# Groups of 8 samples by 64 d in the order of the gather, for a recommendation tower on one core

## The reference

```python
def _cin(x, weights, biases):
    B, F, D = x.shape
    hidden = x
    finals = []
    for i, (w, b) in enumerate(zip(weights, biases)):
        size = w.shape[0]
        z = jnp.einsum('bhd,bfd->bhfd', hidden, x).reshape(B, hidden.shape[1] * F, D)
        y = jnp.einsum('bcd,oc->bod', z, w) + b[None, :, None]
        y = jax.nn.relu(y)
        if i != n_layers - 1:
            hidden, direct = (y[:, :size // 2, :], y[:, size // 2:, :])
        else:
            direct = y
        finals.append(direct)
    return jnp.concatenate(finals, axis=1).sum(-1)
...
h = jnp.concatenate([z, dense_ctx], axis=1)
h = jnp.maximum(h @ W_top1 + b_top1, 0.0)
h = jnp.maximum(h @ W_top2 + b_top2, 0.0)
y = h @ W_top3
```

## Time and profile before

| | |
|---|---|
| three runs | 1093.88, 1093.7, 1091.5 us (median 1093.7) |
| profiled execution, whole | 1092.62 us |
| its span, first to last instruction | 1090.8 us |
| mean granted clock of PE | 0.978 |
| busy: PE / DVE / POOL / ACT | 1025.0 / 944.4 / 915.5 / 734.9 us |
| DMA queue of SP, share of the 16 engines | 70.3%, 192 MB |

### The profile page before, as it was taken

One profiled execution on the slowest core, in us unless ns is written; L12 is line 12 of the kernel. 1 busy time (PEld: TensorE's weight loads), 2 busy tenths in 40 slices (PEclk: granted clock), 3 DMA queues, 4 the chain that ended last, 5 costly groups with the idle time before them and its releaser, 6 DMA issues.

```text
span 1090.8 us, 10701 instructions
## 1 busy us (share of the span) xinstructions
PE 1025.0 (94%) x3493; PEld 651.4 (60%) x3493; DVE 944.4 (87%) x623; ACT 734.9 (67%) x907; POOL 915.5 (84%) x300
## 2 busy tenths in 40 slices
PE   2059999999999999999999999999999999999999
PEld 1025556656666666666666666666666666666664
DVE  4059999999999999999999999999998989888982
ACT  1036666767777677777777777777777777777761
POOL 7526878779999999999999899997989888988890
PEclk9569999999999999999999999999999999999999
DMA  4278777687878787778877878787777877786730
GB/s 137 55 188 200 194 186 184 180 198 190 210 178 205 183 213 187 192 191 199 207 185 192 201 181 208 182 206 194 194 184 194 204 183 187 191 208 184 183 84 1
DMA packets 142074, 196.89 MB, mean 180 GB/s; under 512 B 15858, under 2 KB 57458, under 8 KB 141891
## 3 DMA queue, kind: packets, MB, share of 16 engines
q1 hardware_dynamic: 137922, 192.01, 70.3%
q0 software_dynamic: 4096, 4.20, 1.8%
HBM read 175.18 MB, written 20.97 MB: 180 GB/s over the span
## 4 chain that ended last, share of the span: by engine, by line
PE 86%; DVE 4%; issue 4%; DMA 3%; ACT 2%; SPq 1%; DVEq 0%; ACTq 0%
PE py L610 40%; PE py L626 15%; PE py L616 14%; PE py L617 14%; DVE zf L498 2%; ACT zh L362 2%; PE py L631 1%; DMA xs<-x_dram 1%; DMA x_dram<-xf 1%; DMA xs<-in_L_rec_w 1%; PE pt L592 1%; DVE zl L515 1%; PE py L675 0%; PE pzS L675 0%; DVE zf L459 0%
## 5 line engine op out<-in xcount | busy, mean ns | idle before, releaser
L303 POOL TENSOR_TENSOR zl<-zf,zh 128x2048 fp32r<-128x2048 f32 x168 | 772.3, 4610 | 116.2 <-ACT zh L362 114.2
L498 DVE TENSOR_TENSOR zf<-xs,hid 128x2048 f32<-128x2048 f32 x256 | 583.3, 2283 | 67.1 <-ACT hid L377 51.9
L610 PE MATMUL py<-zf,wf 128*128 128x512 f32 x1072 | 485.2, 596 | 6.5 <-DVE zf L498 6.5
L362 ACT ACTIVATE zh<-zf 128x2048 fp32r<-128x2048 f32 x186 | 354.9, 1908 | 44.5 <-DVE zf L498 41.1
L610 PEld LDWEIGHTS py<-zf,wf 128*128 128x128 f32 x1072 | 203.5, 190 | 214.2 <-issue 194.2
L616 PE MATMUL py<-zh,wh 128*128 128x512 f32 x744 | 293.6, 395 | 8.7 <-ACT zh L362 8.7
L617 PE MATMUL py<-zh,wl 128*128 128x512 f32 x744 | 292.1, 393 | 0.0
L626 PE MATMUL py<-zl,wh 128*128 128x512 f32 x744 | 233.8, 436 | 0.0
L498 DVE TENSOR_TENSOR zf<-xs,px 128x2048 f32<-128x2048 f32 x64 | 146.4, 2288 | 37.8 <-DMA xs<-x_dram 35.9
L626 PEld LDWEIGHTS py<-zl,wh 128*128 128x128 f32 x744 | 135.9, 189 | 59.2 <-issue 29.2
L293 POOL DMA_INDIRECT emb<-in_tbl,idx x128 | 143.1, 1118 | 29.9 <-issue 24.5
(11 more groups left out here) (71 smaller groups left out, 439.8 us busy)
## 6 DMA issues: line engine op xcount, KB each, us to landing
xs<-x_dram SPq DMA_DIRECT2D x640, 256.0 KB
x_dram<-xf SPq DMA_DIRECT2D x64, 320.0 KB
emb<-in_tbl,idx POOLq DMA_INDIRECT x128
xs<-in_L_rec_w SPq DMA_DIRECT2D x2, 512.0 KB
xs<-in_L_rec_w SPq DMA_DIRECT2D x1, 1024.0 KB
wt<-in_W_top SPq DMA_DIRECT2D x1, 512.0 KB
wt1b<-in_W_top SPq DMA_DIRECT2D x1, 256.0 KB
wt1a<-in_W_top SPq DMA_DIRECT2D x1, 128.0 KB
```

The lines of the kernel that those rows point to most:

```text
L303: pool.tensor_tensor(zl[:, q], zf[:, s], zh[:, q].bitcast(F32), ALU.subtract).then_inc(lo["P"], 1)
L362: act.activation(zh[:, q], zf[:, s], ACT.Copy).then_inc(hi, 1)
L498: dve.tensor_tensor(zf[:, slot(u)], left, right, ALU.mult).then_inc(mult, 1)
L610: mm = pe.matmul(y, wf[:, w, h], zf[:, s, h], start=first and h == 0, stop=ends and h == T - 1)
```

## The change

A group is now 8 samples by all 64 d, that is, the layout that a gather leaves. `stage_x`, `turn_x` and `copy_xf` go. Each batch of gathers is stored as it comes (`store_batch`): `x_dram` is now one block per chunk of 128 samples, 160 rows of 32 KB, written in pieces of 256 bytes (one sample's 64 numbers of one field), five copies as before. A group reads from each row its 2 KB, so the rows that it reads lie 32 KB apart. Group 0 of a chunk waits for all stores of the chunk, 17 DMAs for chunk 0 in batches of 12, 12, 6 and 2 fields; later chunks go in batches of three or two fields, one a group. SP's order puts batch g-1's store behind the loads of x0, xt and xd, and it waits there for the batch's gathers. `emb` holds two chunks in place of four.

The sum over d is a reduction of each group's 512 columns to 8 (`sum_1`, `sum_2`), straight from PSUM, in place of adds to accumulators and the later `sum_d`. `py1` has two banks, in place of `pt`.

In group 0, xd is loaded in two halves and product P made in two; PE runs four whole matmuls of weights by weights when px0 is ready and three behind the tail, whose result nobody reads; A of group 0 is whole. SP loads xd of group 1 ahead of x0 of group 1.

The core of the diff, blank lines left out:

```diff
 NC = B // P
-ND = 4
-N = ND * P
-G = NC * D // ND
-GC = D // ND
+NS = 8
+N = NS * D
+G = B // NS
...
 def mode(unit):
     name, g = unit
-    if name in "PD":
+    if name in "PD" or unit == ("A", 0):
...
+FIRST_BATCHES = [(0, 0, 12), (0, 12, 12), (0, 24, 6), (0, 30, 2)]
+PER_PERIOD = [[3] * 10 + [2], [2] * 16, [2] * 16]
+LATER_BATCHES = [(c, sum(PER_PERIOD[c - 1][:i]), n) for c in range(1, NC) for i, n in enumerate(PER_PERIOD[c - 1])]
+BATCHES = FIRST_BATCHES + LATER_BATCHES
+BATCH_SEMS = 4
+STORES = [sum(min(m, REPEATS) for b, _, m in BATCHES if b == c) for c in range(NC)]
+def gathered_count(n):
+    return 16 * sum(BATCHES[i][2] for i in range(n % BATCH_SEMS, n + 1, BATCH_SEMS))
+def batch_of(g):
+    return len(FIRST_BATCHES) + g if g < len(LATER_BATCHES) else None
...
-        emb = sb("emb", [P, F, NC, D])
+        emb = sb("emb", [P, 2, F, D])
...
-            def store_x(k):
-                sp.wait_ge(xf_ready, k + 1)
-                dst = x_dram[k, 0:1, :]
-                sp.dma_start(bass.AP(tensor=dst.tensor, offset=dst.offset, ap=[[N, F], [P, ND], [F * N, REPEATS], [1, P]]),
-                             view(xf, 0, [[0, REPEATS], [1, P]])).then_inc(x_stored, 16)
+            def store_batch(n):
+                c, f, m = BATCHES[n]
+                sp.wait_ge(gathered[n % BATCH_SEMS], gathered_count(n))
+                if m < REPEATS:
+                    for i in range(m):
+                        dst = x_dram[c, f + i:f + i + 1, :]
+                        sp.dma_start(bass.AP(tensor=dst.tensor, offset=dst.offset, ap=[[D, P], [F * P * D, REPEATS], [1, D]]),
+                                     view(emb, (c % 2 * F + f + i) * D, [[0, REPEATS], [1, D]])).then_inc(x_stored[c], 16)
+                else:
+                    for i in range(REPEATS):
+                        dst = x_dram[c, i * F + f:i * F + f + 1, :]
+                        sp.dma_start(bass.AP(tensor=dst.tensor, offset=dst.offset, ap=[[D, P], [P * D, m], [1, D]]),
+                                     emb[:, c % 2, f:f + m, :]).then_inc(x_stored[c], 16)
+            def rows(k, r):
+                return x_dram[k // GC, r:r + 1, N * (k % GC):N * (k % GC) + N]
             def run_of_rows(k, r):
-                src = x_dram[k, r:r + 1, :]
-                return bass.AP(tensor=src.tensor, offset=src.offset, ap=[[N, P], [1, N]])
...
-            def block_rows(k, j, t):
-                src = x_dram[k, 4 * t + j:4 * t + j + 1, :]
-                return bass.AP(tensor=src.tensor, offset=src.offset, ap=[[N, F], [4 * N, T], [1, N]])
+                src = rows(k, r)
+                return bass.AP(tensor=src.tensor, offset=src.offset, ap=[[P * D, P], [1, N]])
+            def block_rows(k, j, t, n=T):
+                src = rows(k, 4 * t + j)
+                return bass.AP(tensor=src.tensor, offset=src.offset, ap=[[P * D, F], [4 * P * D, n], [1, N]])
             def load_x0(k):
-                sp.wait_ge(x_stored, 16 * (k + 1))
+                if k % GC == 0:
+                    sp.wait_ge(x_stored[k // GC], 16 * STORES[k // GC])
...
                     sp.wait_ge(mult, NTH["C", k - 2])
+                if k == 0:
+                    for t in range(0, T, 2):
+                        for j in (0, 2, 1, 3):
+                            sp.dma_start(xd[0][F * j:F * j + F, t:t + 2], block_rows(0, j, t, 2)).then_inc(x_first[t // 2], 16)
+                    return
                 for j in (0, 2, 1, 3):
                     sp.dma_start(xd[k % 2][F * j:F * j + F], block_rows(k, j, 0)).then_inc(xd_in[k % 2], 16)
...
+            for n in range(len(FIRST_BATCHES)):
+                store_batch(n)
             sp.wait_ge(w_turned, 6)
-            store_x(0)
             load_x0(0)
             load_xd(0)
             load_xt(0)
-            store_x(1)
+            load_xd(1)
             load_x0(1)
+            load_xt(1)
             load_xe(0)
-            load_xt(1)
-            load_xd(1)
-            store_x(2)
             for g in range(G):
                 if g + 2 < G:
                     load_x0(g + 2)
                     load_xt(g + 2)
                     load_xd(g + 2)
-                if g + 3 < G:
-                    store_x(g + 3)
+                if g >= 1 and batch_of(g - 1) is not None:
+                    store_batch(batch_of(g - 1))
                 if g + 1 < G:
                     load_xe(g + 1)
...
-            def gather(c, f):
+            def gather(n, i):
+                c, first, m = BATCHES[n]
+                if i >= m:
+                    return
+                f = first + i
+                if i == 0 and c >= 2:
+                    pool.wait_ge(x_stored[c - 2], 16 * STORES[c - 2])
+                if i == 0 and n >= BATCH_SEMS:
+                    pool.wait_ge(gathered[n % BATCH_SEMS], gathered_count(n - BATCH_SEMS))
                 pool.indirect_dma_start(
-                    out=emb[:, f, c, :], out_offset=None, in_=tables[f],
+                    out=emb[:, c % 2, f, :], out_offset=None, in_=tables[f],
                     in_offset=bass.IndirectOffsetOnAxis(ap=idx[:, c, f:f + 1], axis=0),
-                ).then_inc(gathered[c], 16)
...
-                if g + 3 < G:
-                    stage_x(g + 3)
                 high(("C", g))
                 if g >= 1:
                     finish_2(g - 1)
-                if g + 3 < G:
-                    copy_xf(g + 3)
                 high(("B", g))
                 if g + 1 < G:
...
+                if u == ("P", 0):
+                    dve.wait_ge(x0_ready, 1)
+                    for t in range(0, T, 2):
+                        dve.wait_ge(x_first[t // 2], 16 * 4)
+                        half = dve.tensor_tensor(zf[:, slot(u), t:t + 2], xd[0][:, t:t + 2], view(px0, 0, [[0, 2], [1, N]]), ALU.mult)
+                        half.then_inc(mult if t else first_half, 1)
+                    return
                 if name == "P":
...
-            def add_1(k):
+            def sum_1(k):
                 dve.wait_ge(dir1_ready, k + 1)
...
-                    dve.tensor_tensor(s, py1[H:P], s, ALU.add).then_inc(acc1_done, 1)
+                dve.tensor_reduce(zd[H:P, NS * k:NS * k + NS], py1[H:P, k % 2].rearrange("p (b d) -> p b d", d=D),
+                                  AX_X, ALU.add).then_inc(sum1_done, 1)
...
-                dve.tensor_reduce((zd, zsum2)[a][rows, P * c:P * c + P], acc[rows, c % 2].rearrange("p (d b) -> p b d", d=ND),
-                                  AX_X, ALU.add).then_inc(zsum_ready, 1)
+                dve.tensor_reduce(zsum2[:, NS * g:NS * g + NS], py2[:, g % 2].rearrange("p (b d) -> p b d", d=D),
+                                  AX_X, ALU.add).then_inc(sum2_done, 1)
...
             def bank(u):
-                return py1[:] if u[0] == "P" else py2[:, u[1] % 2]
+                return (py1 if u[0] == "P" else py2)[:, u[1] % 2]
             def main(u):
                 name, g = u
                 s, y, first = slot(u), bank(u), name in "PA"
-                if name == "P" and g >= 1:
-                    pe.wait_ge(swapped, 3 * g)
-                    pe.wait_ge(acc1_done, g)
+                if name == "P" and g >= 2:
+                    pe.wait_ge(swapped, 3 * (g - 1))
+                    pe.wait_ge(sum1_done, g - 1)
                 if name == "A" and g >= 2:
-                    pe.wait_ge(acc2_done, g - 1)
+                    pe.wait_ge(sum2_done, g - 1)
                 if mode(u) == "F":
                     ends = name != "P" and closing(g) == u
                     w = WHOLE_NAMES.index(name)
-                    pe.wait_ge(mult, NTH[u])
+                    if u == ("P", 0):
+                        pe.wait_ge(first_half, 1)
+                    else:
+                        pe.wait_ge(mult, NTH[u])
                     for h in range(T):
+                        if u == ("P", 0) and h == 2:
+                            pe.wait_ge(mult, 1)
                         mm = pe.matmul(y, wf[:, w, h], zf[:, s, h], start=first and h == 0, stop=ends and h == T - 1)
                     mm.then_inc(used_whole, 1)
...
             pe.wait_ge(w_low, 3)
-            turn_x(0)
-            turn_x(1)
-            turn_x(2)
+            def warm_up(n):
+                for i in range(n):
+                    pe.matmul(py2[:, 1], wf[:, 0, i % T], wf[:, 1].rearrange("p t n -> p (t n)"), start=True, stop=True)
+            pe.wait_ge(x0_ready, 1)
+            warm_up(4)
             main(("P", 0))
             tail(0)
+            warm_up(3)
...
-            pe.wait_ge(xf_ready, G)
             pe.wait_ge(mult, len(UNITS))
-            pe.wait_ge(zsum_ready, 2 * NC - 1)
+            pe.wait_ge(sum1_done, G)
             for m in range(4):
                 top_1_begin(m)
-            pe.wait_ge(zsum_ready, 2 * NC)
+            pe.wait_ge(sum2_done, G)
             for m in range(4):
                 top_1_end(m)
```

More of the change, by code:

```diff
@@ L17 @@
 NC = B // P
-ND = 4
-N = ND * P
-G = NC * D // ND
-GC = D // ND
+NS = 8
+N = NS * D
+G = B // NS
```

(43 more changed lines are left out.)

95 lines of the change are left out of this document (22 added, 73 removed).

## The result

The change makes the kernel slower: 1101.1 us median (1096.5 to 1104.5, 7 runs) against 1093.3 (1091.5 to 1093.9, 7 runs), a ratio of 1.0068 (95% interval 1.0052 to 1.0083). The forecast was 1081 with a range of 1077 to 1091.

What follows compares the result with a forecast made beforehand. PE was taken as the bound behind an 86.7 us start. -6.6 - 2.4 - 2.0 + 1.9 - 4.0 = -13.1 took 1092.6 to 1079.5, plus 1.1 for the median, about 1081 us; range 1077 to 1091.

Steps and rivals of the forecast that it cites:

- At nothing: Parts of the change priced at no time: py1's two banks, steady-part stores, SP's and POOL's new waits, the end.
- rival (e): Loads at 32 KB row steps: a row 1.34 times as dear makes DMA the bound; 1.4 gives 1131 us; chance 0.04.
- The turns: Removing one PE transpose of x per group returns 0.11 us each, 60 behind the start: -6.6 us.
- the waits before B: Odd groups up to 9: without ACT's xf copy, PE's 0.49 us gap before B goes at 5 places: -2.4 us.
- the old reductions: Two of DVE's 8 old sum reductions lost 1.0 us each in their periods; removing them: -2.0 us.
- rival (b): DVE's new reductions cost 1.07 us, not 0.70, so PE waits in 11 groups: +8, 1088 us; chance 0.08.
- A piece of 256 bytes at 18 ns: Stores of x to memory: each 256-byte piece takes 18 ns of a DMA engine; ends 13 and 28 ns.
- (a): Stores cost 22 to 33 ns a piece, so chunk 0 lands later: 1084 to 1091 us; chance 0.15.
- (d): 256-byte writes dearer than 512-byte ones: from 33 ns a piece the change loses, at 36 ns 1097 us; chance 0.08.
- x0's load at 53.0: Start: group 0's x0 load is issued at 53.0 us, behind chunk 0's stores, 1.9 us later than before.
- From there to D0, 31.6 us: Start: from the issue of x0's load to D of group 0 on PE, 31.6 instead of 35.6 us: -4.0 us.
- (c): PE's 0.11 us per turn isn't given back because ACT, DVE or POOL is next: +6.6, 1087 us; chance 0.05.

Runs made afterwards that it cites:

- e5: The changed kernel without the stores of chunks 1 to 3, every group loading chunk 0's rows: 1085.9 us, ratio to the kernel before 0.9929.
- e1_pitch34: The changed kernel with 2 KB of padding behind each row, rows 34 KB apart instead of 32 KB: 1080.4 us, ratio to the kernel before 0.9889.
- e10: e1_pitch34 with group 0's edits undone: product P in one piece, no matmuls of weights by weights, A split: 1083.4 us.
- e7_all: The changed kernel with rows 34 KB apart, x0 loaded ahead of xe, and two copies of x in memory instead of five: 1077.3 us.

## Why the prediction was wrong

**The step that failed** is a term that the sum doesn't have: the loads moved to rows 32 KB apart, and I put that at nothing without a row that shows it, not even naming it under "At nothing". It stood only as rival (e), at 0.04, with its threshold in the wrong place. I asked when the DMA engines as a whole become the bound, and found 1.34 times a row's time. They never did; the share in the middle is 0.83, and a row takes 135 ns on average with either distance. What broke is a latency, and most of it only beside the stores (e5): the rows of xe ahead of x0 take 5.0 us in place of 4.0, x0 lands 1.2 us later, and the loop over SP, DMA, ACT and DVE, which had been just shorter than PE's period, is longer. The table shows how small the slack is: the steady part of the changed kernel is 991.9 us with 480 rows in 4.3 us, 1005.9 with 5.0. The question would have been: from the landing of which transfer does a loop close, and how much shorter than PE's period is it? The 24.6 us in 22 places for which ACT already waited for x0 before were the hint, and I didn't read them. One of my own signs of being wrong came true: behind the start DVE waited for xs in 11 places, 7.3 us in total, where e1_pitch34 has no such wait.

The Trainium skill ("DMA: Bandwidth & Descriptors", Latency and other measured facts), by which a pitch of 512 KiB runs at full rate and losses begin at 2 MiB, gave me "no loss here". The runs don't agree with what I made of it: 32, 40 and 48 KB cost 21, 9 and 3 us against 34 KB, and the measurement decides.

**The terms**, each against what e1_pitch34 shows, where that loss is absent, and then against after:

- The turns, the waits before B, the old reductions (-6.6, -2.4, -2.0): from D0 to the end 993.1 us forecast, 991.9 in e1 (and 991.3 to 991.9 in seven kernels). Tail and late product stand without a gap (0.63 us to the late product, 0.93 more to the next), and the periods are 15.36 us. Right, with 1.2 us more than I had: in the groups up to 10 two periods together went from 32.4 to 31.4 us, and I had 0.7 of that 1.0. After: 1005.9, all three gains are overlaid.
- Reductions of 0.70: 0.695 and 0.689. Right; rival (b) is out.
- A piece of 256 bytes at 18 ns: 93.3% of 7.0 us on 16 engines for 5695 pieces is 18.3 ns. Right, with some luck, since the 128-byte pieces of the earlier trace rows between which and the 512-byte stores I placed it are loads, of the indices, and not stores; (a) and (d) are out. The Trainium skill ("DMA: Bandwidth & Descriptors", Specifications) has a read-modify-write below 512 bytes; nothing of that price shows here.
- x0's load at 53.0: 54.2 in e1, 56.0 in after. The sign was right, the size too small. The 12,800 pieces from the second batch on moved for 15.8 us in e1 where I had 14.4: they cost 14.7 us, and I gave them the engines alone, while the gathers' packets hold 9.7% of them. The two gathers of chunk 1 that POOL now issues right behind chunk 0's are not the reason: e10, without them, has X as far behind the 32nd gather (9.5 us; 9.7 in e1 and in after). The other 1.7 us in after are the gathers of its profiled execution: the 32nd was issued at 46.24, in e1 at 44.54. The ends of this term are also 0.2 us off: by its own figures 13 and 28 ns give 50.3 and 61.0.
- From there to D0, 31.6 us: 31.2 in e1, right, and undoing the edits to group 0 gives 3.0 back (e10), as worked out. My two parts, 3.0 and 1.3, make 4.3, of which I took 4.0; e1 has 4.4. In after it took 33.6: with the slow rows x0 of group 1 is copied only at 71.47, X + 15.5 where I had X + 14.3, and the relu stands behind it.

By these terms 1079.5 was forecast for the profiled execution; e1_pitch34's took 1079.1. It is that near by luck too, since X was 1.2 us too early and the rest 1.6 us too long. For after, 3.0 (X), 2.0 (X to D0) and 12.8 (D0 to end) come on top: 1097.3. Against e1_pitch34 the last two are 2.4 and 14.0, and they are what the distance costs in this execution; the 1.7 of X are not. So the sum was sound but for one mechanism, and that was worth more than all it had gained. (c) is out too: PE's 0.11 us was given back.

## What to carry to other kernels

When a change alters where rows lie in memory, price the transfers that a loop waits for, not only the share of the DMA engines: find the loop from a buffer's release over the issue, the landing and the engines behind it back to that release, and compare its length with the period of the bound engine. Where rows of a load lie 32 KB apart, one trial with a pad of 256 bytes is worth it; the pad costs nothing. (40 and 48 KB cost time here too, but a small pad was tried at 32 KB only.) And where PE's busy share looks untouched, compare the periods from one group to the next, and the chain.

## What the runs showed of the hardware

- Loads of 2 KB rows from memory slow down at some distances between the rows: 480 rows in 5.0 us at 32 KB (4.6 without stores going on), 4.4 at 40 and 48, 4.3 at 64, 4.1 at 32.25, 4.0 at 34, and 4.0 at 2 KB (before). It isn't the power of two in the distance. The mean time of a row stays the same (135 ns at 32 and at 34 KB); what grows is the part of rows that take long: one in twenty over 329 ns at 32 KB, 189 at 34 KB, 179 at 2 KB (before).
- Stores of 256 bytes cost 18.3 ns each of an engine's time, 512-byte pieces of before about 28, and gathered rows of 256 bytes about 19.
- The issue of a gather, 0.94 us as a rule, took 1.4 to 3.4 us for two or three of the sixth to ninth, and how much differs from one execution to the next: the 34th was issued at 47.03 in e1_pitch34 and at 49.08 in e7_all. A start that hangs on the last gather moves with it by 2 us, in kernels that don't differ there.
